# Which engine requests the key copies of the second attention layer

## The reference, cut to what matters

```
def _L1_xattn_ref(queries, keys, values, Wq, Wk, Wv, Wo):      # 16 heads of 16 features
    q, k, v = split_heads(queries @ Wq.T), split_heads(keys @ Wk.T), split_heads(values @ Wv.T)
    scores = jnp.einsum('bhqd,bhkd->bhqk', q, k) * scale
    attn = jax.nn.softmax(scores, axis=-1)
    ctx = jnp.einsum('bhqk,bhkd->bhqd', attn, v)
    return ctx.transpose(0, 2, 1, 3).reshape(queries.shape[0], -1, D) @ Wo.T
x = x + _L1_xattn_ref(_layernorm(x), ctx_1024, ctx_1024, ...)
x = x + _L1_ffn_ref(_layernorm(x), W, b, V_r, C)
```

## Time and profile before

| | |
|---|---|
| median of three runs | 812.53 us |
| the profiled execution | 806.61 us, its span 804.9 us |
| second layer's loops 0 to 14 | 604 to 776 us of the span |
| TensorE, VectorE, scalar engine, POOL busy | 94%, 59%, 39%, 35% |

### The profile page before, as it was taken

One profiled execution on the slowest core, in us unless ns is written; L12 is line 12 of the kernel. 1 busy time (PEld: TensorE's weight loads), 2 busy tenths in 40 slices (PEclk: granted clock), 3 DMA queues, 4 the chain that ended last, 5 costly groups with the idle time before them and its releaser, 6 DMA issues.

```text
span 804.9 us, 15694 instructions
## 1 busy us (share of the span) xinstructions
PE 753.2 (94%) x5820; PEld 568.4 (71%) x5820; DVE 477.2 (59%) x1102; ACT 313.3 (39%) x559; POOL 278.9 (35%) x296
## 2 busy tenths in 40 slices
PE   7998999999999988999999999999889989999997
PEld 5675556665676555468999998989667666676775
DVE  2457565245734476733444474747668786988744
ACT  1222311241214112114555555554226664554661
POOL 4762714160140050540451343638693122101010
PEclk8899999999999999999999999999999999999999
DMA  9899532442251087551354342453876573763201
GB/s 257 215 301 332 144 106 89 154 120 91 81 163 49 1 304 263 191 174 34 90 125 125 104 103 75 131 141 103 231 200 197 144 220 115 201 169 84 60 3 46
DMA packets 70684, 115.42 MB, mean 143 GB/s; under 512 B 14881, under 2 KB 55842, under 8 KB 68690
## 3 DMA queue, kind: packets, MB, share of 16 engines
q1 hardware_dynamic: 54864, 62.93, 25.5%
q10 hardware_dynamic: 7906, 31.23, 13.9%
q0 software_dynamic: 7840, 20.26, 9.6%
HBM read 85.81 MB, written 28.41 MB: 142 GB/s over the span
## 4 chain that ended last, share of the span: by engine, by line
PE 73%; DVE 14%; ACT 5%; issue 3%; DMA 2%; POOL 1%; ACTq 1%; POOLq 0%; SPq 0%; DVEq 0%
PE ps L1349 13%; PE ps L1015 11%; PE ps L1026 7%; PE ps L1358 6%; PE ps L1036 4%; PE ps L2033 4%; DVE mxh L1679 4%; PE ps L2062 4%; PE ps L2053 3%; PE ps L2026 2%; PE ps L958 2%; PE ps L2008 2%; PE ps L992 2%; PE ps L1046 2%; DVE gluT L465 2%
## 5 line engine op out<-in xcount | busy, mean ns | idle before, releaser
L1349 PE MATMUL ps<-rowsT,w 128*128 128x128 f32 x1120 | 131.2, 276 | 1.4 <-ACT w L1303 0.8
L1679 DVE TENSOR_REDUCE mxh<-ps 112x2 f32<-112x750 f32 x128 | 115.3, 933 | 23.8 <-PE ps L2033 22.4
L1349 PEld LDWEIGHTS ps<-rowsT,w 128*128 128x128 f32 x1120 | 128.0, 192 | 1.9 <-ACT w L1303 1.0
L1892 ACT ACTIVATE d_pT<-ps 125x448 f32<-125x448 f32 x192 | 92.2, 548 | 67.9 <-PE ps L2053 64.4
L1015 PE MATMUL ps<-x1T,sw 128*128 128x448 f32 x256 | 102.8, 548 | 6.3 <-DVE gluT L465 4.9
L1303 ACT ACTIVATE w<-rw 128x1024 f32 x70 | 73.8, 1056 | 55.6 <-PE ps L1349 55.2
L1015 PEld LDWEIGHTS ps<-x1T,sw 128*128 128x128 f32 x256 | 46.9, 190 | 51.6 <-issue 38.1
L2033 PE MATMUL ps<-kst,qst 96*112 96x375 bf16 x256 | 64.7, 339 | 7.8 <-DVE mxh L1679 2.8
L1358 PE MATMUL ps<-rw,h 128*128 x280 | 66.5, 381 | 0.8 <-DVE y L1276 0.8
L1026 PE MATMUL ps<-sw,gluT 128*112 128x256 f32 x256 | 57.8, 381 | 4.3 <-DVE gluT L465 4.3
L325 POOL DMA_INDIRECT xg<-xh_moe,places x32 | 32.8, 1024 | 83.3 <-DVE places L552 49.0
(11 more groups left out here) (237 smaller groups left out, 1221.1 us busy)
## 6 DMA issues: line engine op xcount, KB each, us to landing
kst<-kscr ACTq DMA_DIRECT2D x45, 378.0 KB, 5.2
rw<-in_rw SPq DMA_DIRECT2D x24, 512.0 KB, 10.2
kscr<-ka SPq DMA_DIRECT2D x16, 567.0 KB, 3.5
cT<-in_ctx_t SPq DMA_DIRECT2D x21, 378.0 KB, 5.1
ctxT<-in_ctx_t SPq DMA_DIRECT2D x16, 378.0 KB
ctxn<-in_ctx SPq DMA_DIRECT2D x16, 336.0 KB
qst<-qscr ACTq DMA_DIRECT2D x12, 448.0 KB, 6.5
rows<-xg SPq DMA_DIRECT2D x35, 128.0 KB, 2.1
```

Source lines behind the costliest of these rows:

```text
L1349: last = mm(bank[1 + 2 * q + k][:, block], w12[:, k, c, block], rowsT[:, q, c * P:(c + 1) * P], start=c == 0, stop=c == C - 1)
L1679: V.tensor_reduce(mxh[:, 2 * g:2 * g + 2], ps[0:S, p:p + 2, 0:K], axis=AX_X, op=ALU.max).then_inc(s["s_max"], 1)
L1892: A(pT[:, q % 2, k, :], bank[4 + k][0:KC, 0:QUAD * S], ACT.Exp).then_inc(s["p_ready"], 1)
```

## The change

The keys of batches 4 to 15 are requested by POOL (`keys_behind(b)`: wait until TensorE has finished all transposed scores of batch b, then request the keys of batch b+4). The scalar engine's request at the end of loops 0 to 11 goes. POOL's calls stand between its other work: keys 4 after the gathers of the first two batches, keys 5 after the last gather, keys 6 ahead of `combine`, keys 7 behind it, keys 8 behind the deviation, keys 9 between the two halves of the split of the queries, keys 10 behind it, and keys 11 to 15 behind the bias additions of groups 0 and 1. The arrivals of these keys count on two semaphores of their own. The bytes and the buffers are the same.

```diff
+    def keys_in(b):
+        if b < 4:
+            return s[f"k_in{b}"], 3 * 16
+        return s[f"later_in{b % 2}"], (b // 2 - 1) * 3 * 16
...
     def gpsimd(pool, n):
+        def keys_behind(b):
+            pool.wait_ge(s["st_ps"], (b + 1) * 4 * NKC)
+            load_keys(pool, b + 4)
...
         for j in range(G):
             pool.wait_ge(s["p_ready"], (2 * j + 2) * NKC)
             gather(pool, i, j)
-        combine(i)
+            if j % 2:
+                keys_behind(j // 2)
+        keys_behind(2)
+        combine(i, range(0, 2))
+        combine(i, range(2, G))
+        keys_behind(3)
         rstd_of(pool, n, NORMS["q", i])
+        keys_behind(4)
         split_queries(pool, i)
+        keys_behind(5)
         split_rest(pool, i)
+        keys_behind(6)
         for i in range(NG - 1):
             rstd_of(pool, n, NORMS["f", i])
             add_bias(pool, i)
+            for b in range(4 * i + 7, min(4 * i + 11, B - 4)):
+                keys_behind(b)
...
     def scalar(a):
             exps(b, 3, range(1, NKC))
-            if b + 4 < B:
-                load_keys(a, b + 4)
             if 2 <= b < 4:
                 scaled(NG - 1, range(2 * (b - 2), 2 * (b - 2) + 2))
...
         def arrived(b):
-            t.wait_ge(s[f"k_in{b % 4}"], (b // 4 + 1) * 3 * 16)
+            t.wait_ge(*keys_in(b))
```

More of the change, by code:

```diff
@@ L1395, in second_layer @@
         "f_ps", "fl_ps", "bl_added", "res_ready", "res_out")}
-    s.update({n: pool_semaphore("d_" + n) for n in ("y_in0", "y_in1", "y_in2", "y_in3")})
+    s.update({n: pool_semaphore("d_" + n) for n in ("y_in0", "y_in1", "y_in2", "y_in3", "later_in0", "later_in1")})
     s.update({n: first[n] for n in ("mv_ready", "rstd_ready", "T_ps", "T_ready", "dve", "pool", "cT_in0", "cT_in1", "cT_in2", "wv1_in",
@@ L1477, in late_load @@
         return B + b - NV
+    def keys_in(b):
+        if b < 4:
+            return s[f"k_in{b}"], 3 * 16
+        return s[f"later_in{b % 2}"], (b // 2 - 1) * 3 * 16
     def load_key_copies(eng, b, a):
         eng.dma_start(kst[b % 4][a:DEPTH:3, :, :].rearrange("p h t -> p (h t)"),
-                      kscr[b].rearrange("s (d g) x -> d s (g x)", d=HD)[:, 0:3:2 if a == 2 else 1, :][:, 0:2, :]).then_inc(s[f"k_in{b % 4}"], 16)
+                      kscr[b].rearrange("s (d g) x -> d s (g x)", d=HD)[:, 0:3:2 if a == 2 else 1, :][:, 0:2, :]).then_inc(keys_in(b)[0], 16)
     def load_keys(eng, b):
@@ L1597, in gpsimd, with combine @@
     def gpsimd(pool, n):
-        def combine(i):
-            for j in range(G):
+        def keys_behind(b):
+            pool.wait_ge(s["st_ps"], (b + 1) * 4 * NKC)
+            load_keys(pool, b + 4)
+        def combine(i, js):
+            for j in js:
                 for k in range(2):
```

## The result

The changed kernel took 816.64 us (median of 20 runs) against 812.52 for the kernel before (20 runs). The ratio is 1.0046, 95% interval 1.0025 to 1.0068: 0.46% slower, or 3.7 us. The forecast was 2.2 us slower.

A forecast was written before the change was run, and what follows sets the result against it. The prediction took TensorE, busy 94% of the span, to bound the kernel. Its terms, -1.24 - 0.95 + 0.8 + 0.6 + 1.0 + 2.0 = +2.2 us, on 812.53 gave 814.7 us, range 813 to 817.5 (8 in 10: 809.5 to 818).

The forecast's parts named there:

- Off the scalar engine: Loops 5 to 11: removing the scalar engine's requests gains nothing, since TensorE's own queue of matmuls covers it.
- The ends of loops 2 and 3: TensorE's waits behind the requests and scalings shrink: 1.24 us gained at loop 2, 0.95 at loop 3, 2.2 in all.
- the lateness of keys 5: Keys 5, requested after the last gather, land late for their use at 631.4: 0.6 us lost.
- The clock: Low clock in loop 3 may go with its idle stretch or return elsewhere: booked zero, 1.7 us both ways.
- Loop 1: Keys 4, requested after POOL's second gather of batch 13, land late: 0.8 us lost, range 0 to 2.6.
- Loop 4: Keys 7, requested behind combine, meet values and query loads and land late: 1.0 us lost, range 0 to 3.
- Loop 6: Requests for keys 9 between the split's halves lengthen the scalar engine's wait: TensorE loses 2.0 us, range 1.3 to 3.3.
- Loops 7 to 14: Later keys are requested at the same moment or with over 5 us to spare, keys 12 about in time: nothing booked.
- the third: Rival: POOL's requests hold up VectorE's small operations at loop ends, about half a microsecond in 12 loops: 820 us, chance 0.08.
- The first: Rival: copies come in time and the clock stays up, 2.6 us faster, 809.9 us; chance 0.25.
- The second: Rival: small lateness at loops 1, 2, 4; loop 6 costs what the two ends give: 812.5 us, chance 0.22.

The follow-up runs named there:

- e12: The changed kernel run again without edit, on the chip of e9: ratio 1.0035 to the kernel before.
- e9: The kernel before run again without edit, for a second profile: ratio 0.9970 to the kernel before.
- e8: The changed kernel without the copies of keys 4 to 15 and the waits for them: ratio 0.9982 to the kernel before.
- e6: The kernel before, with the scalar engine scaling first and requesting keys then at the ends of loops 2 and 3: ratio 1.0005 to the kernel before.
- e1: The changed kernel run again without edit: ratio 1.0083 to the kernel before on the same chip.
- e2: The changed kernel with keys 9 requested behind the whole split, not between its halves: ratio 1.0067 to the kernel before.
- e4: The changed kernel with keys 7 requested ahead of the second half of combine instead of behind it: ratio 1.0045 to the kernel before.
- e3: The changed kernel with keys 4 and 5 requested by the scalar engine again: ratio 1.0045 to the kernel before.
- e10: The kernel before with the scalings spread inside loops 2 and 3 instead of behind the requests at their ends: ratio 0.9968 to the kernel before.

## Why the prediction was right

The measured 3.7 us lie in its range and the direction is right, but the number owes much to luck: terms that were off by up to 3.4 us cancelled, and one of 2.1 us was not in the sum. By its own steps, with e12 against e9:

**Off the scalar engine: nothing in loops 5 to 11.** Right, and not only there: e8 without any request has the same loops 7 to 13 as the kernel before.

**The ends of loops 2 and 3: -2.2 us.** The waits of 1.24 and 0.87 us did go. What is late next was missed: `combine` moved onto VectorE's small operations. With it, and with the lateness of keys 5 that I booked beside it (0.60 us for the key copy in e12, 0.6 forecast), loops 2 and 3 gave 0.86, where the sum has 2.2 - 0.6 = 1.6. And the gain did not need POOL: e6 has it with all requests on the scalar engine.

**The clock: zero, with 1.7 either way.** This is the term that was mis-sized. One wait of 1.1 to 1.6 us at loop 5 came in all three profiles of the changed kernel with 6.8 us at the lower level, 3.4 us of work. In the kernel before, its waits up to 1.24 us in these loops were followed by it once in two profiles.

**Loop 1: keys 4 late by 0.8 us, 0 to 2.6.** 2.42 us in e1, 1.97 in e2 and e4, nothing in e12. e3 shows that their place behind the gathers was the cause.

**Loop 4: +1.0 us.** The cause was right (keys, values and query loads meet, e4), the thing waited for was not: the maxima rows, not the keys, whose third copy had landed (667.9 in e12, the wait began at 669.0). Wait 1.09 us in e12; with the clock behind it, loops 4 and 5 were 4.4 us longer.

**Loop 6: +2.0 us, 1.3 to 3.3.** 1.19 us. The mechanism is as forecast: the wait grew by 1.38 us. The loss is just under its range, for the request was too dear in my sum: 0.50 us, not 0.69 with a gap, and three took 1.5 us where I had at least 1.7.

**Loops 7 to 14: nothing.** Right for all but loop 8, which was 0.5 to 0.9 us longer in all eight profiles where POOL requested keys 12 and equal in the other six. The trace shows the scalar engine's three requests for the last queries stretched from 1.88 to 2.56 us and its exponentials late behind them. What stretched them was not tried and stays open:

```profile
717.49 2.56 ACTq L1844 DMA_DIRECT2D qst<-qscr  x3
720.10 0.54 ACT L1913 ACTIVATE d_pT<-ps 125x448 f32<-125x448 f32 x1 [2.07 <-PE ps L2072]
```

**The end of the kernel: not in the sum.** POOL's last DRAIN got shorter with its 36 more requests, and the end with it by 2.1 us. Nothing in the prediction foresaw it. It takes the 5.2 us that e12's loops 2 to 8 lost down to 3.1.

The loops 2 to 8 of e12 are 5.2 us longer than those of e9, loop 1 is 0.8 shorter and the end 2.1: 2.3 us in sum. The runs showed 2.8 (1.0035) on this chip, 3.7 in the first comparison and 6.7 in e1's. So the sign stands and the size is in the range, by a loss in loops 4 and 5 over four times the forecast one and a gain at the end that hides nearly half of it. Each sum of profiles also holds what low clocks it happened to have. Of the rivals, the third mostly fell: in e12 the loops from 9 on are as long as before, and the small operations kept their length beside requests but at the places named above. The first had the right terms but neither landing nor clock on its side; the third copies of keys landed 5.4 to 8.0 us after issue in e1 and e12, where the profile has the landing. The second, nothing to be seen, is excluded by the first comparison and by e1, not by e12 alone.

## What to carry to other kernels

Moving a request to an idle engine is free only if that engine's order of work doesn't delay it: look at what stands ahead of it there (gathers, a sum) and at what stands behind it (half of a split that another engine waits for). Look at the small transfers of the same stretch, too: in the costliest wait it was not the 378 KB copies but three rows of 3.5 KB, in flight beside them, that TensorE waited for. And when a wait goes, look at what the freed work now runs beside: work moved a microsecond earlier here fell on operations that it made more than three times as long. Compare the ends of two profiles as well as their loops: nearly half of what the loops of e12 lost came back there.

## What was not expected of the hardware

TensorE's granted clock fell to the lower level behind waits of about 1 us and cost more than the wait: 1.09 us of waiting and 3.4 us of work lost in e12, 0.91 and 3.4 in e10, but 1.63 and 1.7 in e3. It did not fall behind every such wait: 1.23 us in e9 had none. Whole loops of one program differed by 2 us between executions (loop 1: 9.49 and 11.56 us) with the clock at its higher level. Three plain requests of POOL for 32 long rows each took 1.5 us, less than the scalar engine's 1.9. POOL's DRAIN at the end of the program took between 4.1 and 9.5 us, differing with the number of requests that POOL had made, and ended the kernel in six of the fourteen profiles.
